# Decoder stack on one core: first group's causal mask by TensorE, second group's rows added by GpSimd, and a last stage whose mix is shared by ScalarE and VectorE

## What is computed

```python
# x: 8 x 256 x 256
x = _layernorm(x + _L0_attn_ref(x, ...))      # 16 heads of 64, causal
x = _layernorm(x + _L0_xattn_ref(x, ctx, ...))
x = _layernorm(x + _L0_ffn_ref(x, ...))       # mixture of 8 experts, two for each row, weighted
x = _layernorm(x + _L1_attn_ref(x, ...))      # 16 heads of 16, gated, causal, then an MLP
x = _layernorm(x + _L1_xattn_ref(x, ctx, ...))
x = _layernorm(x + _L1_ffn_ref(x, ...))

# in _L1_attn_ref
scores = einsum('bqhd,bkhd->bhqk', q, k) / sqrt(Dh)
scores = where(tril(ones((T, T))), scores, -inf)
out = einsum('bhqk,bkhd->bqhd', softmax(scores), v)

# _L1_ffn_ref
x_prev = concatenate([zeros, x[:, :-1, :]])
xr = mu_r * x + (1.0 - mu_r) * x_prev
xk = mu_k * x + (1.0 - mu_k) * x_prev
r = sigmoid(xr @ W_r.T)
out = r * (square(relu(xk @ W_k.T)) @ W_v.T)
```

## Time and profile before

| | us |
|---|---|
| median of 3 runs | 1203.19 (1202.64 to 1204.02) |
| the profiled execution, its own time | 1208.58 |
| its span | 1206.8 |
| TensorE busy | 1103.5 (91%) |
| VectorE busy | 722.0 (60%) |
| ScalarE busy | 548.7 (45%) |
| GpSimd busy | 457.3 (38%) |

### The profile page before, as it was taken

One profiled execution on the slowest core, in us unless ns is written; L12 is line 12 of the kernel. 1 busy time (PEld: TensorE's weight loads), 2 busy tenths in 40 slices (PEclk: granted clock), 3 DMA queues, 4 the chain that ended last, 5 costly groups with the idle time before them and its releaser, 6 DMA issues. The chain is left out here.

```text
span 1206.8 us, 20429 instructions
## 1 busy us (share of the span) xinstructions
PE 1103.5 (91%) x6772; PEld 795.2 (66%) x6772; DVE 722.0 (60%) x2206; ACT 548.7 (45%) x1391; POOL 457.3 (38%) x535
## 2 busy tenths in 40 slices
PE   9899989998998997999999977789799899998996
PEld 4476457546744776999999964455565665565874
DVE  1482476348434845656565638658858787946456
ACT  1371265217322824333333337466576557643541
POOL 0160034006300974766666456025332432223022
PEclk9999999999999998999999989689999999999999
DMA  6000200020002033941111154000000100000001
GB/s 207 18 2 1 59 19 1 0 60 19 1 0 60 2 115 119 310 141 53 45 54 45 41 165 126 2 1 23 14 1 17 36 9 19 8 1 19 1 1 35
DMA packets 39997, 55.85 MB, mean 46 GB/s; under 512 B 6758, under 2 KB 32166, under 8 KB 39894
## 3 DMA queue, kind: packets, MB, share of 16 engines
q1 hardware_dynamic: 30598, 39.61, 10.1%
q0 software_dynamic: 3408, 9.31, 2.8%
q10 hardware_dynamic: 5888, 5.64, 1.5%
HBM read 43.76 MB, written 10.78 MB: 45 GB/s over the span
## 5 line engine op out<-in xcount | busy, mean ns | idle before, releaser
L1787 PE MATMUL bank<-words 128*128 128x256 f32 (+3 forms) x872 | 270.1, 461 | 20.4 <-ACT words L2391 3.7
L1787 PEld LDWEIGHTS bank<-words 128*128 128x128 f32 (+1 forms) x872 | 164.8, 196 | 99.2 <-issue 58.9
L464 PE MATMUL bank<-words 128*128 128x512 f32 x384 | 171.6, 595 | 0.1
L409 POOL TENSOR_TENSOR words<-words 128x256 f32<-128x256 f32 (+1 forms) x128 | 102.5, 829 | 151.8 <-DVE words L1090 151.2
L1297 PEld LDWEIGHTS bank<-words 128*128 128x128 f32 x1248 | 145.9, 193 | 3.5 <-ACT words L1333 1.6
L1297 PE MATMUL bank<-words 128*128 128x128 f32 x1248 | 146.4, 276 | 0.9 <-ACT words L1333 0.9
L787 ACT ACTIVATE words<-words 128x128 f32<-128x128 f32 (+1 forms) x256 | 112.8, 443 | 32.1 <-DVE words L923 32.0
L464 PEld LDWEIGHTS bank<-words 128*128 128x128 f32 x384 | 71.2, 191 | 78.6 <-issue 78.3
L779 ACT ACTIVATE words<-bank 128x512 f32<-128x512 f32 x48 | 28.7, 597 | 178.1 <-PE bank L464 178.1
L1348 ACT ACTIVATE words<-words 128x1024 f32 x39 | 41.1, 1057 | 137.1 <-PE bank L1297 98.4
L913 DVE COPY words<-bank 128x512 f32<-128x512 f32 x48 | 33.2, 691 | 92.2 <-PE bank L464 91.9
(11 more groups left out here) (357 smaller groups left out, 2003.5 us busy)
## 6 DMA issues: line engine op xcount, KB each, us to landing
words<-in_w SPq DMA_DIRECT2D x8, 1024.0 KB
y_slots<-words ACTq DMA_DIRECT2D x39, 128.0 KB
words<-in_w SPq DMA_DIRECT2D x8, 512.0 KB
words<-in_x SPq DMA_DIRECT2D x4, 512.0 KB, 4.1
x_rows<-words SPq DMA_DIRECT2D x16, 128.0 KB, 1.8
words<-in_wm SPq DMA_DIRECT2D x2, 1024.0 KB, 7.6
out_x<-words SPq DMA_DIRECT2D x16, 128.0 KB, 1.8
words<-in_xt SPq DMA_DIRECT2D x3, 512.0 KB, 3.8
```

The costliest lines, as they stand in the source:

```text
L409: last = pool.tensor_tensor(part, part, inv[:, j % SLOTS0, :, t:t + 1].to_broadcast([P, 2, P * (t + 1)]), ALU.mult)
L464: last = pe.matmul(bank[c % 2][:, :], w, r, start=k == 0, stop=k == KD - 1)
L1787: last = pe.matmul(out, w, r, start=i == 0, stop=i == len(pairs) - 1)
```

## The change

- The mask of group 0 is a constant `below` (128 x 384: zero, and -1e30 above the diagonal in the two diagonal blocks), which TensorE adds ahead of the scores: for each of a unit's two banks it multiplies it with the identity and starts the sum, and the scores' products are added on top. VectorE's sixteen `minimum` of this group are gone; ScalarE waits for TensorE.
- The second group's expert rows are weighted and added by GpSimd (`scaled_rows`, `summed_rows`) during the second half's preparation, and VectorE makes their statistics ahead of the second half's units. Their normalised rows come from ScalarE behind units 13 and 14, and the turns go into banks 6 and 7 between the last units.
- At the end no difference is made: ScalarE makes `mu * x` out of the bank, VectorE adds `(1 - mu) * x_prev` (`rest`). The keys are mixed ahead of the last product's sum. GpSimd normalises the older group's rows. TensorE does the first half's receptance ahead of the second turn. The last two tiles have their values, results, statistics and root one by one.

```diff
             def scores(g, units, masked=False):
...
+                        last = pe.matmul(bank[n][:, part], ktm[r, odd, k0:k0 + P], qt[r, m, queries],
+                                         start=not masked, stop=keys == P or not masked)
+                last.then_inc(s1m if masked else s1, len(units))
...
+            def masked_scores(j):
+
+                if j >= 2:
+                    pe.wait_ge(s1e, j - 1)
+                for o in range(2):
+                    pe.matmul(bank[2 * (j % 2) + o][:, 0:CAUSAL], ident[:, :], below[:, :], start=True, stop=False)
+                scores(0, (j,), True)
...
-                        scores(0, (PAIRS1 // GB * b + j,))
+                        masked_scores(PAIRS1 // GB * b + j)
                     if j >= 3 and j % 2:
                         weighted(0, QUADS1 // GB * b + (j - 3) // 2)
-            turn_front(1)
+                    if b and j in (7, 8):
+                        turn(1, n4, j - 7, lambda t: xn[:, t, :], bank[j - 1])
```

GpSimd, in the first group's front and at the end:

```diff
+            def scaled_rows(b):
+
+                for t in range(NT)[rows_of(b)]:
+                    for r in range(2):
+                        pool.wait_ge(backed[r * NT + t], 2 * 16)
+                        pool.tensor_scalar(returned(1, r * NT + t), returned(1, r * NT + t), keep["weight"][:, NT + t, r:r + 1], None, ALU.mult)
+                pool.drain()
+
+            def summed_rows(b):
+
+                part = slice(HALF * D * b, HALF * D * b + HALF * D)
+                pool.tensor_tensor(early_rows[0][:, part], early_rows[0][:, part], early_rows[1][:, part], ALU.add)
+                own = keep["x"][:, NT + HALF * b:NT + HALF * b + HALF, :].rearrange("p t d -> p (t d)")
+                pool.drain()
+                pool.tensor_tensor(own, own, early_rows[0][:, part], ALU.add).then_inc(combined, 1)
...
                 for t in range(NT)[rows_of(b)]:
+                    if b:
+                        scaled_rows(t - HALF)
                     pool.wait_ge(turning, t + 1)
                     pool.tensor_tensor(firstrb[:, t, :], firstrb[:, t, :], firstra[:, t, :], ALU.add).then_inc(swung, 1)
+                    if b:
+                        summed_rows(t - HALF)
...
-            for b in range(2):
-                rstd(LAST, n7, b)
-                last_difference(b)
-            for b in range(2):
-                rstd(OTHER, n8, b)
-            for b in range(2):
-                rstd(0, n9, b)
+            rstd(LAST, n7, 0)
+            older_norm(0)
+            rstd(LAST, n7, 1)
+            older_norm(1)
+            rstd(0, n9, 0)
+            for t in rows_of_last:
+                last_rstd(t)
```

ScalarE and VectorE, in the first group's front and at the end:

```diff
-            heads_copy(0, QUADS1 - 2)
-            heads_copy(0, QUADS1 - 1)
-            front_rows(1)
+                if PAIRS1 - 3 <= j < PAIRS1 - 1:
+                    front_rows(1, j - PAIRS1 + 3)
             for b in range(2):
                 front_turned(1, b)
+                heads_copy(0, QUADS1 - 2 + b)
...
+            def scaled_rows_of(b, source):
+
+                for mu, dst in ((MUK, lastxk), (MUR, lastxr)):
+                    for k in range(KD):
+                        last = act.activation(dst[:, k, batch(b)].rearrange("p (t n) -> p t n", t=HALF), turned_rows(bank[source])[:, k, :, :],
+                                              ACT.Copy, scale=cols[:, mu, k:k + 1])
+                    last.then_inc(lastscaled, 1)
...
+            for b in range(2):
+                mix_rows(LAST, b, 4 + b)
+                scaled_rows_of(b, 4 + b)
+                last_activations(b, (6, 0)[b], (7, 2)[b])
...
+            def last_mix(b, mu, dst):
+
+                dve.wait_ge(lastscaled, 2 * b + (1 if mu == MUK else 2))
+                for k in range(KD):
+                    last = dve.scalar_tensor_tensor(dst[:, k, batch(b)], x5t[:, k, b, 0:S], rest[:, mu - MUR, k:k + 1],
+                                                    dst[:, k, batch(b)], ALU.mult, ALU.add)
+                last.then_inc(lastmixed, 1)
...
+            statistics(OTHER, n8, rows_of_tiles(0))
             normalise(LAST, n7, lambda t: x(LAST, t), 0)
             add_product(LAST, n7, 2, bank[0])
+            last_mix(0, MUK, lastxk)
             add_product(LAST, n7, 3, bank[2])
-            last_mix(0)
+            last_mix(0, MUR, lastxr)
             normalise(LAST, n7, lambda t: x(LAST, t), 1)
+            last_squares(0, 6)
             older_result(1)
```

More of the change, by code:

```diff
@@ L1468, in last_layers @@
         kept = m1t[:, :, :].rearrange("p c n -> p (c n)")
+        below = cut(kept, (G - 1) * (KD * GB * S2 + GB * D), (CAUSAL,))
         keptk, keptv = cut(kept, 0, (G - 1, KD * GB * S2)), cut(kept, (G - 1) * KD * GB * S2, (G - 1, GB * D), S2)
@@ L1530, in rows_of @@
             return slice(HALF * b, HALF * b + HALF)
+        rows_of_last = range(HALF, NT)
         def batch(b):
@@ L1643, in constants @@
                 pool.memset(mask1[:, :], 3e38)
+                pool.memset(below[:, :], 0.0)
                 pool.memset(maskx[:, :], 0.0)
@@ L1651, in constants @@
                 pool.memset(va[:, :, :, DH1:DH1 + 1], 1.0)
+                for c in (slice(0, P), slice(S, CAUSAL)):
+                    pool.affine_select(out=below[:, c], in_=below[:, c], compare_op=ALU.is_ge,
+                                       fill=-1e30, base=0, pattern=[[1, P]], channel_multiplier=-1)
                 pool.affine_select(out=mask1[:, :], in_=mask1[:, :], compare_op=ALU.is_ge,
@@ L1753, in last_bias, with last_rstd, older_norm @@
                 last.then_inc(lastbias, 1)
-            def last_difference(b):
-                pool.wait_ge(n7.copied, 2 * LAST + b + 1)
-                pool.tensor_tensor(lastrl[:, :, batch(b)], x5t[:, :, b, 1:S + 1], x5t[:, :, b, 0:S], ALU.subtract).then_inc(lastapart, 1)
+            def last_rstd(t):
+                pool.wait_ge(n9.stats, t)
+                pool.tensor_tensor(n9.var[:, t:t + 1], n9.mv[:, t:t + 1, 1], eps[:, t:t + 1], ALU.add)
+                pool.drain()
+                pool.tensor_tensor(n9.inv[:, t:t + 1], n9.var[:, t:t + 1], minus_half[:, 0, t:t + 1], ALU.pow).then_inc(n9.rstd, 1)
+            def older_norm(b):
+                rstd(OTHER, n8, b)
+                pool.drain()
+                for t in range(HALF * b, HALF * b + HALF):
+                    pool.tensor_scalar(x(OTHER, t), x(OTHER, t), n8.mv[:, t, 0:1], n8.inv[:, t:t + 1], ALU.subtract, ALU.mult).then_inc(n8.normed, 1)
             pool.wait_ge(n6.turned, 2 * OTHER + 2)
@@ L1828, in form, with scores @@
                 product(bank[4 + i % 2][:, :], [(w[:, k, tok(c % 2)], xnt[:, k, :]) for k in range(KD)]).then_inc(fmm, 1)
-            def scores(g, units):
+            def scores(g, units, masked=False):
                 q = units[0] // 2
@@ L1841, in scores @@
                         k0 = m * GT + b * S + keys
-                        last = pe.matmul(bank[n][:, part], ktm[r, odd, k0:k0 + P], qt[r, m, queries], start=True, stop=True)
-                last.then_inc(s1, len(units))
+                        last = pe.matmul(bank[n][:, part], ktm[r, odd, k0:k0 + P], qt[r, m, queries],
+                                         start=not masked, stop=keys == P or not masked)
+                last.then_inc(s1m if masked else s1, len(units))
             def weighted(g, q):
@@ L2340, in _ @@
             last_receptance(1, 2)
-            last_values(1, 5)
+            pe.wait_ge(lastkact, 2)
+            for t in rows_of_last:
+                product(bank[LASTVALUE[t]][:, 0:D], [(lastrl[:, k, tok(t)], wv2[:, k, :]) for k in range(KD)]).then_inc(lastv, 1)
         @block.scalar
@@ L3045, in _ @@
             first_factors(1)
-            for j in range(PAIRS1 // GB, PAIRS1):
-                minimum(0, j)
-                combine(1, j - PAIRS1 // GB)
-            front_statistics(1)
-            front_normalise(1)
+            for b in range(2):
+                dve.wait_ge(combined, b + 1)
+                front_half(1, b)
+            for b in range(2):
+                front_rows_of(1, b)
             for p in range(1, PERIODS):
@@ L3262, in _ @@
             add_product(LAST, n7, 1, bank[7])
+            statistics(OTHER, n8, rows_of_tiles(0))
             normalise(LAST, n7, lambda t: x(LAST, t), 0)
             add_product(LAST, n7, 2, bank[0])
+            last_mix(0, MUK, lastxk)
             add_product(LAST, n7, 3, bank[2])
[L3266 removed]
+            last_mix(0, MUR, lastxr)
             normalise(LAST, n7, lambda t: x(LAST, t), 1)
+            last_squares(0, 6)
             older_result(1)
[L3269 to L3279 removed]
+            statistics(OTHER, n8, rows_of_tiles(1))
+            last_mix(1, MUK, lastxk)
+            last_mix(1, MUR, lastxr)
+            first_result(4)
+            last_squares(1, 0)
+            last_statistics(rows_of_tiles(0))
+            for t in rows_of_last:
+                last_result(t)
+            for t in range(NT):
+                dve.wait_ge(n9.rstd, max(t, 1))
```

(1 more changed line is left out.)

73 lines of the change are left out of this document (26 added, 47 removed).

## The result

The changed kernel took 1207.54 us (median of 12 runs, 1204.17 to 1211.64), the kernel before 1203.62 in the same comparison (12 runs): 1.0039 times as long, 95% interval 1.0025 to 1.0054. By that ratio it is 4.7 us slower (3.0 to 6.5); the two medians differ by 3.9 us. The forecast was +1.5 us.

A forecast was written before the change was run, and what follows sets the result against it. TensorE, busy for 91% of the span, was taken as the bound, also of the attention stage once it masks. Part 1 +4.6 and part 2 -3.1 gave +1.5 us on the median of 1203.19: 1204.7 us, range 1200.0 to 1209.0.

The forecast's parts named there:

- The mask's price: First group's attention: two mask products 1.29 us plus scores 0.86, so a unit costs TensorE 2.15 us against 1.75.
- part 1: First group's attention stage, mask moved to TensorE and second group's rows to GpSimd: +4.6 us.
- pause to the second half: Between the batches of eight units: copy of heads 0.4 us, then 5.93 less 0.5 for transposes at full clock.
- to the next stage's first product: Behind the second batch: turn, copies, last weighted sums, turned heads and handovers, 4.2 us, first product at 797.7.
- The clock: Pause between the batches: one fall, some 3 us of the second batch's start at half speed, +1.6 us.
- The rival of a clock that stays full: Both attention batches at full clock: clock's term 0, sum -0.1 us, 1203.1; chance 0.10.
- The rival of a clock that stays low for longer: Attention: a fall at the start and a longer one in the gap, sum +4.0 us, 1207.2; chance 0.20.
- The scores for their columns alone: Single unit's scores between masks take 0.645 us instead of 0.86: sum -1.9, 1201.3; chance 0.20.
- GpSimd: Second group's weighted rows end at 762 to 767 us, before VectorE asks at 774: hidden.
- The end: Part 2, the chain round the engines in the last 23 us: -3.1 us, bounds -1.5 to -4.
- The rival of GpSimd in the way of the first mix: End: GpSimd's older-group normalisation costs each VectorE mix up to 1.2 us; sum +3.1, 1206.3; chance 0.15.
- The signs: Expected in the trace: next stage's first product at 797 to 800, VectorE idle in the attention stage, ScalarE never waiting for it.

The follow-up runs named there:

- the doubled masks: The changed kernel with each mask product made twice in a row, four 384-column products per unit instead of two: 1229.47 us (one run).
- what happened with bfloat16: The changed kernel with the mask's product (constant and identity) in bfloat16: 1206.49 us, ratio to the kernel before 1.0005 to 1.0032.
- the kernel with the minimum back: The changed kernel with VectorE's minimum masking the first group again, all else of the change kept: 1197.70 us, ratio to the kernel before 0.9943 to 0.9973.
- the last experiment: The changed kernel with VectorE's minimum back and GpSimd's second turning sum ahead of its adding of rows: 1202.24 us, ratio to the kernel before 0.9974 to 0.9993.
- a pair of float32 units: The changed kernel with bfloat16 masks except float32 in units 8 and 9: 1199.60 and 1206.65 us; with GpSimd's rows later as well, 1194.63 us.

## Why the forecast was right in sign and off in size

**The mask's price was the step that failed.** "So a unit costs TensorE 2.15 us": it costs 2.34. That TensorE pays for the masks stood; this term was too small. Both parts that were priced came near: scores between masks were priced at 0.86 and take 0.85; a product's columns were priced at 0.645 and the doubled masks show 0.64. Missing was 0.2 us for each block of masks (1.49 instead of 1.29), 16 times, 3.0 us in all with the scores' 0.01 taken off. The range had an upper bound for the scores, and none for the mask, which was in no row; I should have given it one.

The rest of the ledger of part 1, in us:

| step | forecast | measured |
|---|---|---|
| first half, to the end of its last weighted sums but one | 19.6 | 21.09 |
| pause to the second half | 5.9 | 5.87 |
| second half without the clock | 19.6 | 21.09 |
| clock | +1.6 | +1.37 |
| to the next stage's first product | 4.2 | 4.48 |
| that product at full clock, not partly low | -0.5 | -0.46 |
| GpSimd and VectorE in each other's way | +0.2 | hidden |
| against before | +4.6 | +7.45 |

(Halves: 748.18 to 768.48 + 0.79, and 775.14 to 797.60 = 22.46 with the clock's 1.37, which is 2.86 - 1.49. The last but two: the profiled stretch from the next stage's start to its first table load is 27.71 us instead of 28.17. 53.90 - 45.99 - 0.46 = 7.45.)

**The clock**: one fall, in the pause, back after one block of masks; as forecast, and no more. The rival of a clock that stays full falls: 2.93 in the row at 775.14. The rival of a clock that stays low for longer falls for this kernel, in both its profiles, and names what happened with bfloat16. Two of the kernel's thirteen executions were profiled; the others' mean clocks (0.979 to 0.986, profiles 0.982 and 0.984) leave room for a second fall somewhere.

**The scores for their columns alone** (0.645, the rival on the faster side): falls, 0.85.

**GpSimd**: hidden, as forecast; it ended at 766.2, VectorE asked behind 770. It did slow VectorE (two scans 2.30 us, where the kernel with the minimum back has 1.41), and it cost nothing, since VectorE then waits for ScalarE (12.86 us, up to 770.58):

```profile
753.81 2.30 DVE L3042 TENSOR_TENSOR_SCAN words<-words 128x256 f32<-128x256 f32 x2
```

The Trainium skill (GPSIMD Engine Reference, Key points) has GpSimd share SBUF interfaces with two-input instructions of VectorE; the scans here and in the last experiment, which have two and lie beside GpSimd's additions, agree. Beside its multiplications by a weight the traces don't decide: VectorE's 128x512 sum took 0.71 there in one kernel (761.75, minimum back) and 1.16 in another (751.02, mask in bfloat16). And the 128x64 operation of the earlier trace rows, 0.70 us beside an addition, has a single input from SBUF; in the changed kernel it took 0.23 (752.72).

**The end**: -3.1 forecast, -3.17 measured. Counted from the copy of the first turned rows, the steps came as worked out: keys' product 2.64 forecast and 2.74 measured, second turn 6.3 and 6.42, Relu 11.7 and 11.91, end of the last normalisation 19.3 and 19.33. The rival of GpSimd in the way of the first mix falls: 0.87 us, with 0.8 forecast.

**The signs.** The next stage's first product was to come at 797 to 800 and came at 802.08, the missing 0.2 us a unit again. VectorE was to be idle in the stage and was busy for 18.26 us; but ScalarE waited for it only once, 0.42 us at 771.31, and none of the exponentials did.

**The sum**: +7.45 - 3.17 = +4.3, beside +4.7 (3.9 by the medians) measured over the runs. Laying the forecast onto the median and not onto the profiled execution was right, since the latter held 6 us more in a stretch that the change doesn't touch. What stays open is when the clock falls, in that stretch and in the first half.

## What to carry to other kernels

An operation that is moved onto an engine which then bounds the stage can cost more than it frees: 16 blocks of masks by 1.49 us made the stage 10.5 us longer (53.90 instead of 43.39), for what VectorE did in 10.9 us beside other work. When such a move is tried, try its companions alone too; here each of the two others was a gain (2.6 us in the stage, 3.2 to 5.9 over the runs), and the loss of the third hid both. Price an operation between two others with a bound for the change-over. Where single profiles differ in a stretch that nobody touched, compare marks within the stages.

## What the runs showed of the hardware

- A block of 384-column float32 products by the whole array, ahead of score products by 32-row groups, takes 0.21 us more than its columns up to their start (1.49 for two, 2.77 for four), behind an idle TensorE as behind scores.
- TensorE without a gap is not enough for the full clock: 1.2 GHz from 769.66 to 792.65 with the mask in bfloat16. In the second half the full clock came back within a unit in all four profiled executions with float32 masks throughout, in none of two with bfloat16 alone, and within the pair in two of three with a pair of float32 units. But behind a first half of bfloat16 masks at 1.2 GHz it was full at the turns (771.05 and 771.12, 1.17 us for eight) in both profiles that had one, and low again by the next unit. I can't say from this what decides it.
- The same program can have its first half at 2.4 GHz in one execution and at 1.2 in another: with bfloat16 masks it fell at 750 in two of five profiles. With float32 masks it fell in the first half in none of four, with VectorE's minimum (and TensorE waiting between the units) in all five, at 751 to 753.
- The same 380 us of work took 379.2 us in the profile in which the clock never fell there and 387.7 in the one with 14.6 us at 1.2 GHz, near 874, 915, 1051 and 1099 us, where TensorE was busy in 3.40 of 3.40, 3.40 of 3.40, 3.30 of 3.30 and 3.14 of 3.30 us of the windows over them.
